# Seven projections of the next batch, each run in two pieces of two chunks among the feed-forward tiles

## The reference

```
x = LN(x + causal_attention(x, Wq, Wk, Wv, Wo))         # stage A, 16 heads, windows of 512
x = LN(x + cross_attention(x, ctx))                     # stage B
x = LN(x + base(x) + gated_lora(x))                     # stage C
x = LN(x + flow_attention(x))                           # stage D
x = LN(x + plain_attention(x, ctx, ctx))                # stage E
h = bit_linear(x, w1); h = silu(depthwise_conv3(h))     # stage F, 512 -> 2048
x = LN(x + bit_linear(h, w2))                           # stage F, 2048 -> 512
```

## Time and profile before

| | |
|---|---|
| median of 3 runs | 2627.15 us (2626.56 to 2629.21) |
| profiled execution | 2629.23 us, span 2627.4 us |
| PE busy | 2365.7 us, 90% |
| DVE, ACT, POOL busy | 1579.9, 1245.8, 687.0 us |
| mean granted clock of TensorE | 0.977 |
| tiles of stage F, first `f_g` to last: batch 0, batch 3 | 563.6 to 677.2 us, 2488.8 to 2593.0 us |

### The profile page before, as it was taken

How to read it: one execution, slowest core, us unless ns; L and a number is a source line. 1 busy time by engine, 2 the same in 40 slices (tenths; PEclk the granted TensorE clock), 3 DMA queues, 4 the chain that set the end, 5 groups by cost and what they waited for, 6 DMA issues and landing times.

```text
span 2627.4 us, 37008 instructions
## 1 busy us (share of the span) xinstructions
PE 2365.7 (90%) x12984; PEld 1311.6 (50%) x13000; DVE 1579.9 (60%) x3101; ACT 1245.8 (47%) x2870; POOL 687.0 (26%) x989
## 2 busy tenths in 40 slices
PE   7889999988988999998898999988889899999867
PEld 3655544445465544444556554444455655444344
DVE  4664633468866462447877655165787746516688
ACT  5753312258675422127868341222886823122396
POOL 0002221026401232013720213101480021310266
PEclk9999999999999999999999999999999999999888
DMA  8001101010210200001030110001003010100000
GB/s 298 18 10 50 46 20 33 0 49 1 85 52 10 71 29 17 32 1 49 9 127 2 47 34 29 32 17 43 7 9 127 2 57 23 45 1 1 0 1 33
DMA packets 58987, 99.41 MB, mean 38 GB/s; under 512 B 13364, under 2 KB 13748, under 8 KB 58296
## 3 DMA queue, kind: packets, MB, share of 16 engines
q1 hardware_dynamic: 58808, 97.06, 11.2%
HBM read 88.66 MB, written 8.39 MB: 37 GB/s over the span
## 4 chain that ended last, share of the span: by engine, by line
PE 63%; DVE 16%; ACT 15%; issue 4%; POOL 0%; DMA 0%; ACTq 0%; DVEq 0%; POOLq 0%; SPq 0%
PE psum L396 22%; PE psum L390 17%; ACT prob L801 6%; PE psum L474 3%; DVE neg_max L1095 3%; PE psum L540 2%; DVE f_a L1102 2%; PE psum L782 2%; ACT xT L829 1%; PE psum L754 1%; DVE f_top L1382 1%; DVE f_g L1372 1%; PE psum L560 1%; ACT f_z L997 1%; PE psum L611 1%
## 5 line engine op out<-in xcount | busy, mean ns | idle before, releaser
L390 PE MATMUL psum<-xT,weights 128*128 128x512 f32 x1152 | 508.9, 595 | 16.6 <-DMA weights<-in_a_k 10.3
L390 PEld LDWEIGHTS psum<-xT,weights 128*128 128x128 f32 x1152 | 214.9, 191 | 265.7 <-issue 246.6
L396 PE MATMUL psum<-weights,mixed 128*128 128x512 f32 x768 | 338.8, 597 | 0.0
L801 ACT ACTIVATE prob<-psum,neg_max 128x128 f32<-128x128 f32 (+3 forms) x512 | 264.9, 543 | 109.6 <-DVE neg_max L1095 109.6
L396 PE MATMUL psum<-weights,xT 128*128 128x512 f32 x640 | 289.0, 596 | 2.4 <-DVE recip L1285 1.6
L1420 POOL TENSOR_SCALAR var<-stats 128x1 f32<-128x1 f32 x192 | 61.1, 318 | 792.5 <-DVE stats L1046 792.5
L1095 DVE TENSOR_REDUCE neg_max<-psum 128x1 f32<-128x128 f32 (+3 forms) x512 | 217.0, 481 | 81.3 <-PE psum L479 46.6
L1433 POOL TENSOR_TENSOR f_a<-f_a,f_z 128x256 f32<-128x256 f32 x256 | 199.6, 788 | 133.6 <-DVE f_a L1102 127.0
L396 PEld LDWEIGHTS psum<-weights,mixed 128*128 128x128 f32 x768 | 144.4, 191 | 179.8 <-issue 179.0
L1076 DVE TENSOR_TENSOR x<-psum,x 128x512 f32<-128x512 f32 x128 | 88.3, 690 | 225.3 <-PE psum L396 163.2
L829 ACT COPY xT<-psum 128x512 f32<-128x512 f32 x128 | 67.1, 596 | 327.7 <-PE psum L427 327.7
(11 more groups left out here) (242 smaller groups left out, 4034.1 us busy)
## 6 DMA issues: line engine op xcount, KB each, us to landing
xT<-in_xT SPq DMA_DIRECT2D x8, 1024.0 KB, 6.3
x<-in_x SPq DMA_DIRECT2D x8, 1024.0 KB, 8.8
out<-x SPq DMA_DIRECT2D x16, 512.0 KB, 2.8
weights<-in_a_k SPq DMA_DIRECT2D x4, 1024.0 KB, 5.4
weights<-in_a_q SPq DMA_DIRECT2D x4, 1024.0 KB, 5.1
weights<-in_a_v SPq DMA_DIRECT2D x4, 1024.0 KB, 5.0
w1f<-in_w SPq DMA_DIRECT2D x4, 1024.0 KB, 14.8
w2f<-in_w SPq DMA_DIRECT2D x4, 1024.0 KB, 17.3
```

The source lines that it names most:

```text
L390: last = mm(bank[:, 0:n], weights[weight][:, c, heads(g)], rhs(c), start=(c == 0), stop=(c == C - 1))
L396: last = mm(bank, lhsT(c), weights[weight][:, c, :], start=(c == 0), stop=(stop and c == C - 1))
L801: last = run(sb["prob"][:, slot, o:o + keys], bank[:, o:o + keys], ACT.Exp, bias=sb["neg_max"][:, n, qc, j:j + 1], accum_out=sb["a_sum"][: ...
```

## The change

The seven projections that stood after n = 14, 21, ..., 56 are each split into two pieces of two chunks, and the 14 pieces stand after n = 12, 16 | 20, 24 | 27, 31 | 35, 39 | 43, 46 | 50, 54 | 58, 62. The first piece claims the bank and starts the accumulation, the second ends it and raises the semaphore; ACT copies at the place of the second piece. The other five projections keep their places. `a_project` and `a_projected` hold the code that the steps `a_key`, `a_query` and `a_value` had.

```diff
     if b < B - 1:
-        for n, step in zip((2, 3, 5, 6, 14, 21, 28, 35, 42, 49, 56, 64), FIRST_PROJECTIONS):
+        for n, step in zip((2, 3, 5, 6, 64), FIRST_PROJECTIONS[:4] + FIRST_PROJECTIONS[-1:]):
             at.setdefault(n, []).append(("next", step))
+        for i, n in enumerate((12, 16, 20, 24, 27, 31, 35, 39, 43, 46, 50, 54, 58, 62)):
+            at.setdefault(n, []).append(("next", ("a_half", *FIRST_PROJECTIONS[4 + i // 2], i % 2)))
...
+            def a_project(name, chunks):
+
+                kind, n = name
+                ring = query_ring(n) if kind == "a_query" else act_ring
+                g, w = divmod(n, W) if kind == "a_query" else (n, 0)
+                if 0 in chunks:
+                    weight_ready(pe, {"a_key": "a_k", "a_query": "a_q", "a_value": "a_v"}[kind])
+                    xT_ready(pe, 0, n if kind == "a_value" else WT * w + WT - 1)
+                    if name == ("a_query", Q_SLOTS) and now[0] > 0:
+                        pe.wait_ge(q["f_out_taken"], at("f_out_taken", 0))
+                    bank = ring.claim(pe, name)
+                else:
+                    bank = ring.bank(name)
+                for c in chunks:
+                    if kind == "a_value":
+                        last = mm(bank, xT[:, c, heads(n)], weights["a_v"][:, c, :], start=(c == 0), stop=(c == C - 1))
+                    else:
+                        last = mm(bank, weights["a_k" if kind == "a_key" else "a_q"][:, c, heads(g)], xT[:, c, tokens(w)],
+                                  start=(c == 0), stop=(c == C - 1))
+                if C - 1 in chunks:
+                    last.then_inc(ring.filled, 1)
...
+                elif kind in ("a_key", "a_query", "a_value"):
+                    a_project(step, range(C))
+                elif kind == "a_half":
+                    name, n, half = arg
+                    a_project((name, n), range(C // 2 * half, C // 2 * (half + 1)))
...
+                elif kind in ("a_key", "a_query", "a_value"):
+                    a_projected(step)
+                elif kind == "a_half" and arg[2] == 1:
+                    a_projected((arg[0], arg[1]))
```

More of the change, by code:

```diff
@@ L803, in exponentials, with a_projected @@
                     last.then_inc(a_ring.freed, 1)
+            def a_projected(name):
+                kind, n = name
+                if kind == "a_query":
+                    run(query(n), query_ring(n).take(act, name), ACT.Copy, scale=SCALE).then_inc(query_ring(n).freed, 1)
+                else:
+                    copy(sb["a_k" if kind == "a_key" else "a_v"][:, n, :], act_ring.take(act, name)).then_inc(act_ring.freed, 1)
             def load_table(i, function):
```

## The result

The changed kernel takes 2606.83 us in the median of 6 runs (2605.63 to 2611.18), the kernel before 2627.57 us in 6 runs. The ratio is 0.9924, 95% interval 0.9914 to 0.9935: faster by 20.7 us, clear of the 0.2% that a measurement tells from no change. The forecast was 2617.2 us, its range 2608 to 2627. The profiled execution has a span of 2605.3 us against 2627.4, 22.1 less.

A forecast was written before the change was run, and what follows sets the result against it. The prediction took ACT, nearly full and to be kept fed, to bound stage F. ACT's savings of 3.3 us in three batches, 9.9 us, with seam and clock at 0, took the median 2627.15 to 2617.2 us, range 2608 to 2627.

The forecast's parts named there:

- What bounds the stage: Stage F: projections cost 7.0 us a batch, mostly in tiles 14 to 40; ACT's idle time is where gain must come from.
- The seam at 0: Between projection pieces and bf16 tiles: seven extra seams priced at 0, at most 0.16 us each, 1.1 us a batch.
- DVE's waits: DVE waiting for PE's tiles behind projections: 2.21 us after 21 falls to 0.5, 1.84 at 28 to 0.1.
- What ACT wins: ACT's waits in stage F: 1.25 + 1.75 + 0.3 = 3.3 us saved a batch.
- the five near the projections: ACT's five waits near projections at 21, 28 and 35, together 2.06 us, fall to 0.3, saving 1.75.
- the last three: ACT's last three waits, together 3.0 us, belong to `f_out` and the third chain and stay.
- natural ceiling: Stage F's gain: 3.5 us a batch, 10.5 us in all, unless the clock or a chain gives more.
- a price of 0: PE's granted clock in stage F: expected 1.00 again, since PE work is kept and spread more evenly; cost 0.
- rival A: Behind the last tile the clock may hold, 1.7 us more a batch, and ACT's waits vanish: 2609 us; chance 0.20.
- B: Stage F: ACT, POOL or the chains absorb most; 3 us in all left, 2624 us, within 0.2%; chance 0.20.
- C: Pieces from 35 on, where PE lacks slack, cost DVE about 1.5 us each: slower, 2636 us; chance 0.10.
- D: Split leaves 1.72 us of dense work; clock falls in three 3.4 us stretches a batch: 2632 us; chance 0.05.

The follow-up runs named there:

- x1: Kernel before with the seven projections still whole, moved to after n = 12, 20, 27, 35, 43, 50, 58: 2641.48 us, ratio 1.0055.
- z1: Kernel before with spare matmuls that nobody reads in four of PE's pauses a batch (stage B, two in stage D, behind the last tile): 2616.81 us, ratio 0.9957.
- x3: Changed kernel, but only the last four of the seven projections split, the first three whole at 14, 21, 28: 2624.82 us, ratio 0.9993.
- x4: Changed kernel with all seven split, but the two pieces after n and n + 1, one tile between them: 2623.54 us, ratio 0.9986.
- w3: As w1 (changed kernel, first four projections moved too), but without the spare matmuls: 2610.79 us, ratio 0.9936.
- x2: Changed kernel, but only the first three of the seven projections split, the other four whole at 35, 42, 49, 56: 2627.06 us, ratio 0.9995.
- w1: Changed kernel with four groups of spare matmuls in PE's pauses, and the first four projections moved too: 2602.2 us, ratio 0.9902.

## Why the prediction missed, step by step

**What bounds the stage: right.** Tiles 14 to 40 carry most of the gain, ACT is what must be fed, and the loss was PE's late tiles: the earlier trace rows against the waits above, and x1, where the waits of 2 us return.

**The seam at 0: right.** Timeline of PE in the changed kernel, the second piece of a projection (after n = 24) and the tile behind it:

```profile
604.86 1.88 PE L424 MATMUL psum<-xT,weights 128*128 128x512 f32 x4
606.58 0.60 PE L763 MATMUL psum<-f_xqT,w 128*128 128x258 bf16 x4
```

From start to start 1.72 us, exactly half of the 3.44 of a whole projection.

**DVE's waits: right.** The wait after 21 was to fall from 2.21 to nearly nothing with a piece at 20, and the one behind an odd place to 0.5: no wait stands behind the piece at 20, and 0.49 us behind the one at 27.

**"What ACT wins", 3.3 us a batch: the mechanism right, the term 1.4 too small.** ACT's waits fell by 4.8 us, tile 63 comes 4.1 us earlier and the first `f_out` behind it 4.7. In three batches that is 4.1 us more than the forecast. The prediction left too much standing: the wait at the first chain went from 1.66 to 0, not to 0.4; the five near the projections and the two near 42 went to 0, not to 0.3 each; the second chain's fell from 1.05 to 0.69. Of the last three, 3.0 us together, 2.8 stayed (the third chain's fell from 1.39 to 0.92, while one of `f_out`'s rose from 0.92 to 1.39). I suppose that batch 3 was the wrong yardstick for the chains: its ACT has no copies to make in a chain, while in batches 0 to 2 the copies are work that fills it; in the changed kernel a copy stands in each of the first two (609.35 and 632.46 us). The "natural ceiling" of 3.5 us a batch was too low as well.

**The clock "a price of 0": the step that failed.** "I expect 1.00 again and a price of 0" held for tiles 14 to 63 and was false for the program. I looked at the clock in the stage that changes, and in one place behind it (rival A, 1.7 us a batch; the tail gave 0.6). I did not look at the 528 us between the tiles of two batches, where the kernel before runs a second stretch at half clock in every batch. In place of 0 the clock was worth 0.6 us behind the last tile and 1.5 in stage B, 2.1 a batch. Ahead of batch 0 the kernel before has the two stretches of stage D at half clock and the changed one has neither, 2.8 us, of which a later start in the first 31 us takes 1.0 back. Together 3 x 2.1 + 1.8 = 8.1 of the 22.1 us between the two profiled executions. The sum of the prediction with both corrections is 9.9 + 4.1 + 8.1 = 22.1; with the first alone, 14.0, the time would have lain within the stated range. z1 shows the clock without the change: filling the pauses gives 10.6 us.

**The rivals.** A came nearest, with 2609 us. It was right that the pause behind the last tile shrinks to about 1 us (0.93) and that the clock then holds, but this is worth 0.6 us a batch and not 1.7; the 1.5 that lies in stage B, which A did not name, makes the total come out. That part of its agreement is luck. B is out: neither ACT nor POOL absorbed the gain. C is out: behind 43 and 46 DVE waits 0.68 us and less. D is out: 1.00 up to tile 63. The Trainium skill ("TensorE: Matmul & The Clock Gate", section "Why this matters for your kernels") advises for thin matmuls, with M under 512, to run all chunks of a contraction before the next DMA, or else the clock swings at every chunk. That does not speak against this split: what stands between the pieces is other matmuls and no wait for a DMA, and the granted clock is 1.00 in all of the tiles from 590 to 672.

**What stays open.** Why the clock falls behind one pause of 2.50 us and not behind the next (x3) is not shown. It is the same code, and counted from tile 63 the two batches reach the pause within 0.3 us of each other. Within an execution the batches mostly repeat it (x3, x4 and w3 change once), so that its price often comes three times: before, and in x2 with tiles 2.5 us shorter, a batch takes the same 641.7 us (1205.3 - 563.6, 1203.4 - 561.7). Two of the six runs of the changed kernel lie at 2611.1 us with a mean clock of 0.980, four at 2605.6 to 2607.1 with 0.982; without a profile of those two I can only suppose that they have one stretch more a batch. So the 20.7 us are measured, but some 7 of them (8 of the 22.1 in the traces) are not shown to be a property of this change, and another edit of a few us elsewhere may give them back, as x2 and x3 did.

## What to carry to other kernels

Work for the next stage that PE does among the tiles of this one should come in pieces that cost the next engine little (here 1.72 us, 0.7 us of wait at most, against 3.44 us and waits of about 2), with some tiles between them (3 to 5 here; one was not enough); moved as a whole it costs what it cost, or more (x1). When an edit of a few microseconds stands in a program that repeats, compare the stretches that the edit doesn't touch as well, with their granted clock, before the difference is put down to the edit. If PE's pauses are the cause, a few spare matmuls in them bring two kernels closer to comparable, and may be worth keeping; look even then at the pauses that were not filled, as stage E in z1 and w1 shows.

## What the runs showed of the hardware

The same eight transposes behind the same pause of 2.50 us took 1.21 us at one time, at a granted clock of 1.00, and 1.95 at another of the same execution, at 0.52. A stretch of 3.4 us at half clock cost the program 0.6 to 1.6 us, by its place. Spare matmuls of 0.22 us in four pauses of a batch made a program of 2627 us 10.6 us shorter; more of them in the pauses of stage E made one of 2605 us 13 us longer. Splitting an accumulation over three to five tiles, with other matmuls in other banks between, cost nothing that a row shows: 1.72 us from the first matmul of a piece to the next tile, half of the 3.44 of the whole.
